# Four and three staging slots instead of two for the residual tiles of the layer-1 epilogues, some of them loaded on GpSimd's queue

## What is computed

```python
x = x + 0.5 * L0_ffn(layernorm(x))    # silu(x Wg) * (x Wu), then Wd; inner width 8192
x = x + L0_attn(layernorm(x))         # tanh(x B^T) C^T + D * x; 1024 states
x = x + 0.5 * L0_ffn(layernorm(x))
x = x + 0.5 * L1_ffn(layernorm(x))    # selects one of 8 low-rank experts for each token
x = x + L1_attn(layernorm(x))         # projections, causal conv, a scan along the tokens, W_out
x = x + 0.5 * L1_ffn(layernorm(x))
```

## Time and profile before

| | us |
|---|---|
| median of 2 runs | 8107.95 |
| the two runs | 8092.76 and 8123.14 |
| the profiled execution | 8092.76 |
| its span on the slowest core (core 6) | 8091.3 |
| spans of the other cores | 8017.1 to 8089.6 |
| mean granted TensorE clock, all cores | 0.882 to 0.888 of 2.4 GHz |

### The profile page before, as it was taken

The page is one execution under the profiler, slowest core; times in us unless marked ns, Lnnn a source line. Parts: engine busy times, 40 slices in busy tenths (PEclk is TensorE's granted clock), DMA queues, the critical chain, the costliest instruction groups (busy, mean ns, idle before and its releaser), DMA issues.

```text
span 8091.3 us, 70297 instructions; the slowest of 8 cores (8017.1 to 8091.3 us)
## 1 busy us (share of the span) xinstructions
PE 6461.8 (80%) x27794; PEld 2774.8 (34%) x28341; DVE 1504.2 (19%) x2253; ACT 742.5 (9%) x1164; POOL 362.5 (4%) x654
## 2 busy tenths in 40 slices
PE   4999999996996977669999999979799544454344
PEld 1444444442442423224444444434344110121110
DVE  4100100100000023250010010000000433523443
ACT  2000000000000011020000000000000200220200
POOL 1000000001000000000000000010000000000000
PEclk8999999998998988889999999989899765676655
DMA  4323333335556552822222222255655413323413
GB/s 63 58 58 58 57 58 58 56 59 128 115 114 159 114 99 46 185 53 57 56 60 56 57 60 55 58 146 116 146 128 116 72 56 98 65 41 110 88 58 108
DMA packets 260180, 676.59 MB, mean 84 GB/s; under 512 B 26624, under 2 KB 78976, under 8 KB 243472
## 3 DMA queue, kind: packets, MB, share of 16 engines
q0 software_dynamic: 120832, 353.22, 26.4%
q1 hardware_dynamic: 79120, 193.00, 6.6%
q10 hardware_dynamic: 59904, 125.86, 6.1%
HBM read 840.60 MB, written 167.77 MB: 125 GB/s over the span
## 4 chain that ended last, share of the span: by engine, by line
PE 71%; DVE 12%; DMA 12%; issue 2%; ACT 1%; SPq 1%; DVEq 0%; POOL 0%; ACTq 0%; POOLq 0%
PE ps L268 43%; PE ps L355 11%; PE ps L353 11%; DVE RESG L56 5%; DVE XBF L56 4%; DMA RESG<-res_a 3%; DMA res_b<-RESG 2%; DMA BIGB<-h_scr 2%; PE ps L409 1%; PE ps L768 1%; DMA RESG<-res_b 1%; DMA res_a<-RESG 1%; SPq L128 1%; DVE TMPF L56 1%; DVE BIGB L56 1%
## 5 line engine op out<-in xcount | busy, mean ns | idle before, releaser
L268 PE MATMUL ps<-XBF,WBUF 128*128 128x512 bf16 x16056 | 3528.2, 380 | 78.0 <-DVE XBF L56 60.6
L268 PEld LDWEIGHTS ps<-XBF,WBUF 128*128 128x128 bf16 x16384 | 1604.7, 98 | 2000.9 <-issue 73.9
L353 PE MATMUL ps<-BIGB,WBUF 128*128 128x512 bf16 x1966 | 749.8, 381 | 262.7 <-DMA BIGB<-h_scr 262.7
L56 DVE TENSOR_TENSOR HEV<-TMPF,ps 128x512 bf16<-128x512 f32 x512 | 352.2, 688 | 3175.5 <-PE ps L268 3134.4
L355 PE MATMUL ps<-BIGB,WBUF 128*128 128x512 bf16 x2048 | 780.5, 381 | 4.3
L355 PE MATMUL ps<-XBF,WBUF 128*128 128x512 bf16 x2048 | 776.2, 379 | 4.3
L353 PE MATMUL ps<-XBF,WBUF 128*128 128x512 bf16 x1967 | 745.5, 379 | 0.0
L56 ACT ACTIVATE TMPF<-ps 128x512 f32<-128x512 f32 x512 | 305.7, 597 | 3178.2 <-PE ps L268 3141.3
L56 ACT ACTIVATE HEV<-XBF 128x512 bf16<-128x512 bf16 x384 | 241.8, 630 | 2571.2 <-DMA XBF<-res_a 2205.7
L201 PE MATMUL ps<-HEV 128*128 128x512 bf16 x384 | 176.4, 459 | 349.9 <-ACT HEV L56 323.1
L56 DVE SCALAR_TENSOR_TENSOR RESG<-ps,RESG 128x512 f32<-128x512 f32 x128 | 88.6, 692 | 1947.1 <-PE ps L355 1940.5
(11 more groups left out here) (144 smaller groups left out, 2017.9 us busy)
## 6 DMA issues: line engine op xcount, KB each, us to landing
WBUF<-wgu POOLq DMA_DIRECT2D x256, 512.0 KB, 6.0
WBUF<-wdn POOLq DMA_DIRECT2D x128, 1024.0 KB, 9.7
h_scr<-HEV SPq DMA_DIRECT2D x128, 512.0 KB, 4.8
RESG<-res_a ACTq DMA_DIRECT2D x192, 256.0 KB, 3.5
res_a<-RESG SPq DMA_DIRECT2D x64, 512.0 KB, 9.3
res_b<-RESG SPq DMA_DIRECT2D x128, 256.0 KB, 3.8
XBF<-res_a POOLq DMA_DIRECT2D x48, 512.0 KB, 23.2
BIGB<-h_scr POOLq DMA_DIRECT2D x64, 256.0 KB, 25.4
```

The lines of the kernel that those rows point to most:

```text
L56: instr = attr(*a, **k)
L268: last = t.matmul(banks[tc][:], wsl[:, k * 128:(k + 1) * 128], XBF[:, k * T + tc * TC: k * T + (tc + 1) * TC], start=(k == 0), stop=(k == ...
L353: t.matmul(b0[:], wsl[:, ib * 128:(ib + 1) * 128], hsrc[:, 0:512], start=st_, stop=sp_)
```

## The change

The L1-FFN epilogue uses all four slots of RESG instead of two; slots 0 and 2 are loaded on ACT's queue, slots 1 and 3 on POOL's, each with a semaphore of its own (`rslg`). Since these slots include the columns that the layer norm writes, ACT and POOL wait for the end of the layer norm before the first tile of the first chunk. The L1-attention epilogue uses three slots (columns 512 to 2047) instead of two; slot 1 is loaded on POOL's queue. The PSUM banks stay two in both. Stores stay on SP's queue. The barrier waits for the two new semaphores too.

```diff
@@ P.__init__
+        self.rslg = [Sem(nc, f"rslg{i}") for i in range(2)]
@@ emit_l1ffn
-        dg = {"ev0": 0, "ev1": 0, "st0": 0, "st1": 0}
+        dg = {"ev0": 0, "ev1": 0, "st0": 0, "st1": 0, "st2": 0, "st3": 0}
...
             t.wait_ge(self.sc.h, sc_fgb)
+            if tc == 0:
+                self.nc.scalar.wait_ge(self.ev.h, self.ln_done)
+                self.nc.gpsimd.wait_ge(self.ev.h, self.ln_done)
             for dblk in range(NK):
                 bank = self.ps[2 + (dblk % 2)]
+                rs = dblk % 4
...
-                rslot = self.RESG[:, (dblk % 2) * TC:(dblk % 2 + 1) * TC]
-                if dg["st" + str(dblk % 2)]:
-                    self.nc.scalar.wait_ge(self.ssl[dblk % 2].h,
-                                           dg["st" + str(dblk % 2)])
-                rtok = self._dma(self.nc.scalar, self.rsl[dblk % 2], rslot,
+                rslot = self.RESG[:, rs * TC:(rs + 1) * TC]
+                ldq = self.nc.gpsimd if rs % 2 == 1 else self.nc.scalar
+                lsem = self.rslg[rs // 2] if rs % 2 == 1 else self.rsl[rs]
+                if dg["st" + str(rs)]:
+                    ldq.wait_ge(self.ssl[rs].h, dg["st" + str(rs)])
+                rtok = self._dma(ldq, lsem, rslot,
                                  res_src[dblk * 128:(dblk + 1) * 128, cs])
                 v.wait(self.mm, mm_d)
-                v.wait(self.rsl[dblk % 2], rtok)
+                v.wait(lsem, rtok)
...
-                dg["st" + str(dblk % 2)] = self._dma(
-                    q, self.ssl[dblk % 2],
+                dg["st" + str(rs)] = self._dma(
+                    q, self.ssl[rs],
                     res_dst[dblk * 128:(dblk + 1) * 128, cs], rslot)
@@ emit_l1attn
-        wo_st = [0, 0]
+        wo_st3 = [0, 0, 0]
...
                 slot = dblk % 2
+                rs = dblk % 3
...
-                rslot = self.RESG[:, 1024 + slot * TC: 1024 + (slot + 1) * TC]
-                if wo_st[slot]:
-                    self.nc.scalar.wait_ge(self.ssl[slot].h, wo_st[slot])
-                rtok = self._dma(self.nc.scalar, self.rsl[slot], rslot,
+                rslot = self.RESG[:, 512 + rs * TC: 512 + (rs + 1) * TC]
+                ldq = self.nc.gpsimd if rs == 1 else self.nc.scalar
+                lsem = self.rslg[0] if rs == 1 else self.rsl[rs]
+                if wo_st3[rs]:
+                    ldq.wait_ge(self.ssl[rs].h, wo_st3[rs])
+                rtok = self._dma(ldq, lsem, rslot,
                                  res_src[dblk * 128:(dblk + 1) * 128, ccs])
...
-                v.wait(self.rsl[slot], rtok)
+                v.wait(lsem, rtok)
...
-                wo_st[slot] = self._dma(
-                    q, self.ssl[slot],
+                wo_st3[rs] = self._dma(
+                    q, self.ssl[rs],
                     res_dst[dblk * 128:(dblk + 1) * 128, ccs], rslot)
@@ barrier_all
-                self.ssl + self.hsl)
+                self.rslg + self.ssl + self.hsl)
```

## The result

| us | before | after |
|---|---|---|
| executions compared | 8092.8 and 8123.1 | 7905.7 and 7914.5 |
| ratio, with its 95% interval | | 0.9756 [0.9674, 0.9838] |
| all executions, median | 8864.62 (12) | 8795.26 (14) |
| predicted | | 7850, range 7775 to 7935 |

What follows compares the result with a forecast made beforehand. The store, load and VectorE round on two RESG slots was taken to bound the L1 epilogues, 697 us. Gains of 199 (FFN) + 67 (attention) - 13 (between) = 253 us from 8092.8 give 7840, 7855 on the median; predicted 7850, range 7775 to 7935.

Steps and rivals of the forecast that it cites:

- (a): L1-FFN epilogue with four slots: 2.35 us a tile, 34.8 us an epilogue, eight of them 199 us less than 477.
- (d): L1-attention epilogue with three slots, slot 1 on POOL: a turn of 7.5 us, 38.2 us an epilogue, 67 us less.
- The other estimate: Price of an FFN tile from the L0-attention epilogue: 2.9 us there, 2.4 us without its weight loads.
- (b): L1-FFN slots 1 and 3 loaded on POOL's queue: landing about 1 us later than ACT's, no gain from the queue.
- (c): ACT and POOL waiting at the first chunk for the end of the layer norm: costs nothing.
- (e): Work after some epilogues starts from TensorE's last product, so two tiles' gain there is off the path: 13 us.
- the crowded case: Rival, both epilogues: DMAs crowd as in L0-attention, 2.9 us a tile, 7912 us (7927 on the median), chance 0.12.
- the main case: FFN epilogues at 2.1 to 2.7 us a tile, 7820 to 7895 us on the median's basis, chance 0.55.
- Unhindered DMAs: Rival, both epilogues: DMAs hardly slow down, 1.87 us a tile in FFN, 2.3 in attention, 7785 us, chance 0.17.
- Starved loads: Rival: POOL's loads wait out 3.06 us of VectorE work, 3.1 us a tile in FFN, 7906 us, chance 0.07.
- the slower case: Rival, both epilogues: POOL's loads land after 24.4 us, 596 us more, 8690 us; decides from 11 us; chance 0.03.
- the stall only moves: Rival: store and load together take 11.6 us; 107 us gained in FFN, none in attention, about 7990 us, chance 0.06.

## Where the prediction was right, and which step of it failed

**What bounds the kernel.** Right. The round of store, load and VectorE on a slot was the limit: more slots shorten the epilogues, a queue alone does not, and each part alone gives its own share. The step that failed is the price of a tile in (a) and of a turn in (d), how much the DMAs slow each other down: 2.35 us a tile was taken and 2.58 measured, a turn of 7.5 us was taken and 8.2 measured.

**(a) FFN, the term that was mis-sized most.** The mechanism was right: four slots crowd the DMAs. The price of a tile was taken as 2.35 us and is 2.58: 37.5 us an epilogue where 34.8 was forecast, 177 us gained instead of 199. It came from the busy share of L0-attention, 2.0 us of full DMA time a tile at a share of 0.85, and both numbers were wrong: with four slots it is 1.7 us a tile at a share of 0.67 (0.61 over the whole first epilogue). That 2.35 comes within a tenth of 2.58 is therefore partly luck: the two errors cancel in part, and the right 1.7 at a share of 0.85 would have given 2.0. Four slots did not fill the engines, and the turn still grew, from 7.9 to 10.3 us. A share is no measure of how much faster the slots can turn. The other estimate, 2.4 us from 2.9 without the weights, was too low as well.

**(b) POOL's queue.** Half right. It gains nothing, and its loads are not starved behind VectorE: once issued they land in 3.9 us, ACT's in 4.1, so the 1 us of later landing does not exist. In its place stand the 0.48 us between release and issue, which is on the path whenever that slot sets the turn. The allowance of 7.8 us for store and load was too small by what crowding added: in the turn shown above they take 3.77 + 4.51 us and 0.5 us of hand-over, 8.8 us in all.

**(c) The waits at the first chunk.** Forecast to cost nothing, and never tested alone: the first epilogue starts 4.1 us later, on two different cores of two executions, and the spans of the four cores of after already differ by 42 us. Whether the waits have a part in it can't be told.

**(d) Attention.** Three slots: a turn of (41.9 - 0.7) / 5 = 8.2 us, not 7.5. It is the same error as in (a): 0.6 us was allowed over today's 6.9, and the VectorE rows show 1.3 (7.1 to 8.4). The gain is 49 us on these two cores instead of 67, 38 by the medians.

**(e) Between the epilogues.** The sign was right and the mechanism too, the size too small: 23 us on these two cores instead of 13, 18 by the medians. In before TensorE went on at 6617.4 us while VectorE ended its epilogue at 6624.4, 7.0 us later; in after it is 3.0 us. Core 6 of before, then core 3 of after:

```profile
6617.43 5.13 PE L565 MATMUL ps<-XBF,WBUF 128*64 128x512 bf16 x16
```

```profile
6601.25 4.97 PE L566 MATMUL ps<-XBF,WBUF 128*64 128x512 bf16 x16
...
6602.82 1.48 DVE L56 TENSOR_TENSOR RESG<-RESG,ps 128x512 f32<-128x512 f32 x2 [0.72 <-DMA RESG<-res_a]
```

So 3.9 us of that gain lay beside TensorE's next work, not 2.8: a mean price per tile was used, and the last tiles of an epilogue had been slower than the mean (turns of 8.3 to 8.5 us against 7.9). By the start and end of each epilogue the four such hand-overs in FFN grew by 3.7, 4.9, 0.5 and 4.8 us and the one in attention by 5.2. Of the other 4 us, 3.2 lie between attention and the last FFN stage and 1.2 before the last attention epilogue, places where the prediction had nothing; their cause was not looked for.

**The sum.** 22 us short in FFN, 18 in attention, 10 between, 4 at the start: 54 of the 253 us did not come. Three quarters is one mis-sized term, the crowding.

**The rivals.** Nearest in time was the crowded case (7912 to 7927 us), at 2.9 us a tile; by the tile (2.58) the main case (2.1 to 2.7) holds in FFN, while in attention 8.2 / 3 = 2.7 us lies between its 2.5 and the rival's 2.9, nearer to the rival. Unhindered DMAs fell with the landing times. Starved loads fell with POOL's 3.9 us, and with them the slower case, which needed 11. That the stall only moves fell with the halved wait. Of the predicted signs the wait for loads (216 for about 200), ACT's landing (4.1 for 4 to 5) and the epilogues' order of size came; POOL's landing (3.9 for 5) and the DMA share (0.61 for 0.7 to 0.85) did not. One sign that the prediction itself had called proof of being wrong did occur: the time between epilogues grew, from 828 to 851 us. The sign was badly chosen, since (e) forecasts 13 us of such growth.

## What to carry to other kernels

More staging slots in a load, compute, store round bring less than their number says: here each further slot made the turn 0.7 to 1.4 us longer, so measure the turn at two slot counts, in the same way, before pricing a third. Slots that can be filled ahead, in the idle time between two bursts, are worth more than slots that only deepen the burst: eight instead of four brought 84 us here, with the DMA rate in the burst up only from 192 to 221 GB/s. And read the wait before the first block of every loop for which instance of a token it names.

## What the runs showed of the hardware

- Landing times of 256 KB float32 tiles grow with how many are in flight although the DMA engines are not full: medians over these epilogues of 3.3, 3.6, 4.1 and 4.8 us for loads on ACT's queue and 2.4, 3.1, 3.6 and 4.3 us for stores, with two, three, four and eight slots, at a busy share of 0.43, 0.57, 0.67 and 0.84.
- The packets themselves take the same time at every slot count: 86 to 88 ns for 2 KB of a store, 117 to 130 ns for 2 KB of a load on ACT's queue, 1.7 us of full DMA time for the load and store of a tile.
- A load on POOL's queue lands no later than one on ACT's beside VectorE's float32 work (3.9 and 4.1 us); it is issued 0.48 us after its release, ACT's within 0.07.
- Loads weigh more than twice as much as stores: half the loads took 5.9 us off an epilogue, half the stores 2.4.
